# Threshold search of a router: the missed bit kept in PSUM and folded into the next candidate by one operation

## The reference

```python
probs = softmax(einsum('bsd,ed->bse', x, choice_w), axis=-1)
G, I = jax.lax.top_k(jnp.swapaxes(probs, -1, -2), k)
x_in = take_along_axis(x[:, None, :, :], I[..., None], axis=2)
h = silu(einsum('bekd,edf->bekf', x_in, w1))
x_mlp = einsum('bekf,efd->bekd', h, w2)
out = zeros_like(x).at[b_idx, I].add(G[..., None] * x_mlp)
```

## Time and profile before

| what | value |
|---|---|
| median of 3 runs | 2411.73 us (2411.46 to 2414.36) |
| profiled execution | 2411.47 us, of which the span from first to last instruction is 2409.6 us |
| PE (TensorE) busy | 2364.5 us, 98% of the span |
| DVE (VectorE) busy | 1401.0 us, 58% |
| ACT (ScalarE) busy | 839.1 us, 35% |
| POOL (GpSimd) busy | 1106.8 us, 46% |
| mean granted clock of TensorE | 0.996 |

### The profile page before, as it was taken

How to read it: one execution, slowest core, us unless ns; L and a number is a source line. 1 busy time by engine, 2 the same in 40 slices (tenths; PEclk the granted TensorE clock), 3 DMA queues, 4 the chain that set the end, 5 groups by cost and what they waited for, 6 DMA issues and landing times.

```text
span 2409.6 us, 34867 instructions
## 1 busy us (share of the span) xinstructions
PE 2364.5 (98%) x12586; PEld 2006.1 (83%) x12586; DVE 1401.0 (58%) x2730; ACT 839.1 (35%) x1470; POOL 1106.8 (46%) x980
## 2 busy tenths in 40 slices
PE   7999999999999999999999999999999999999997
PEld 6899978888999888888888888888888888888886
DVE  7777788967776888643543543543543544444433
ACT  4455444444454445322322322322223223223222
POOL 2000024400000246666566665665665665765765
PEclk9999999999999999999999999999999999999998
DMA  7555433445453434622522522522523423423322
GB/s 189 168 120 157 121 61 53 56 95 161 121 146 99 76 55 70 152 51 45 121 48 46 119 47 45 120 45 48 120 44 53 116 44 64 104 46 72 94 44 44
DMA packets 128139, 209.66 MB, mean 87 GB/s; under 512 B 28728, under 2 KB 53944, under 8 KB 127808
## 3 DMA queue, kind: packets, MB, share of 16 engines
q0 software_dynamic: 57728, 119.09, 27.6%
q1 hardware_dynamic: 70336, 89.68, 12.9%
HBM read 124.54 MB, written 100.93 MB: 94 GB/s over the span
## 4 chain that ended last, share of the span: by engine, by line
PE 93%; DVE 5%; ACT 1%; issue 1%; DMA 1%; POOL 0%; SPq 0%; DVEq 0%; ACTq 0%; POOLq 0%
PE ps L1291 30%; PE ps L1292 29%; PE ps L1293 29%; PE ps L1387 2%; PE ps L1519 1%; PE ps L1318 1%; DVE work L1229 0%; DVE thr L1141 0%; DVE stats L785 0%; DVE work L1212 0%; DMA xo<-in_L_attn_x_dram 0%; DMA normed_rows<-xo 0%; DVE qT L1004 0%; PE ps L1505 0%; DVE xT_lo L846 0%
## 5 line engine op out<-in xcount | busy, mean ns | idle before, releaser
L449 POOL DMA_INDIRECT rows<-normed_rows,idx_row x528 | 563.7, 1068 | 209.0 <-issue 209.0
L1291 PE MATMUL ps<-xi_hi,w_hi 128*128 128x512 f32 x1024 | 404.3, 395 | 0.0
L1291 PE MATMUL ps<-w_hi,h_hi 128*128 128x512 f32 x1024 | 402.3, 393 | 0.0
L1292 PE MATMUL ps<-xi_lo,w_hi 128*128 128x512 f32 x1024 | 400.4, 391 | 0.0
L1292 PE MATMUL ps<-w_lo,h_hi 128*128 128x512 f32 x1024 | 399.4, 390 | 0.0
L1293 PE MATMUL ps<-w_hi,h_lo 128*128 128x512 f32 x1024 | 399.1, 390 | 0.0
L1293 PE MATMUL ps<-xi_hi,w_lo 128*128 128x512 f32 x1024 | 398.7, 389 | 0.0
L1259 DVE CAST h_hi<-hf 128x512 fp32r<-128x512 f32 x256 | 111.5, 436 | 411.2 <-ACT hf L748 410.9
L546 POOL DMA_INDIRECT out_dram<-y,idx x128 | 221.4, 1730 | 273.1 <-ACT y L767 260.3
L748 ACT ACTIVATE hf<-ps 128x512 f32<-128x512 f32 x256 | 153.1, 598 | 519.4 <-PE ps L1293 519.4
L1293 PE MATMUL ps<-wq_hi,xT_lo 128*128 128x256 f32 (+2 forms) x768 | 246.4, 321 | 0.0
(11 more groups left out here) (174 smaller groups left out, 4217.4 us busy)
## 6 DMA issues: line engine op xcount, KB each, us to landing
w_raw<-in_L_ffn_w_dram SPq DMA_DIRECT2D x36, 512.0 KB, 8.1
w_raw<-in_L_ffn_w_dram SPq DMA_DIRECT2D x9, 2048.0 KB, 9.1
xo<-in_L_attn_x_dram SPq DMA_DIRECT2D x32, 512.0 KB, 4.5
normed_rows<-xo SPq DMA_DIRECT2D x32, 512.0 KB, 4.7
out_dram<-bo POOLq DMA_DIRECT2D x16, 1024.0 KB, 9.2
out_dram<-xo POOLq DMA_DIRECT2D x64, 256.0 KB, 3.9
xn<-normed_rows SPq DMA_DIRECT2D x96, 128.0 KB, 2.4
rows<-normed_rows,idx_row POOLq DMA_INDIRECT x528, 2.6
```

What stands on the lines that cost most here:

```text
L449: nc.gpsimd.indirect_dma_start(rows[:, tt, a, :], None, pieces[:, :], bass.IndirectOffsetOnAxis(ap=idx_row[:, b, tile, a:a + 1], axis=0)). ...
L1291: nc.tensor.matmul(dst, a_hi, b_hi, start=start, stop=False, skip_group_check=True)
L1292: nc.tensor.matmul(dst, a_hi, b_lo, start=False, stop=False, skip_group_check=True)
```

## The change

`hit` is gone. Its place takes `miss`, the last column of PSUM bank 7, seen as int32: it holds the bit if the count fell short, and zero if it did not. The candidate is kept over the steps: it starts as the highest bit, and one operation makes the next one from it, `cand = (miss | bit[s+1]) ^ cand`, which takes the missed bit out and puts the next one in. Behind the last bit `thr = miss ^ cand`. Each step so has one VectorE instruction and one wait fewer (60 in the two batches), and of the operation that follows the test one tensor lies in PSUM.

```diff
             thr = sb("thr", [P, 1], I32)
             cand = sb("cand", [P, 1], I32)
-            hit = sb("hit", [P, 1], I32)
+        miss = ps[:, 7, 511:512].bitcast(I32)
...
                     me.did(nc.vector.tensor_copy(probT, ps[:, 7, 0:2 * P]))
-                    me.did(nc.vector.memset(thr[:, :], 0))
+                    me.did(nc.vector.tensor_copy(cand[:, :], bit[:, 0:1]))
                     me.wait()
...
                 def count(s):
-                    me.did(nc.vector.tensor_tensor(cand[:, :], thr[:, :], bit[:, s:s + 1], ALU.bitwise_or))
-                    me.wait()
                     nc.vector.tensor_scalar(mark, probT, cand[:, :].bitcast(F32), None, ALU.is_ge, ALU.add,
                                             accum_out=cnt[:, 0:1]).then_inc(route_dve, 1)
...
                 def settle(s):
                     dve.wait_ge(route_pe, b * ROUTE + s + 2)
-                    me.did(nc.vector.tensor_scalar(hit[:, :], ps[:, 7, 0:1], float(CAP) - 0.5,
-                                                   bit[:, NT + s:NT + s + 1].bitcast(F32), ALU.is_ge, ALU.mult))
+                    me.did(nc.vector.tensor_scalar(miss, ps[:, 7, 0:1], float(CAP) - 0.5,
+                                                   bit[:, NT + s:NT + s + 1].bitcast(F32), ALU.is_lt, ALU.mult))
                     me.wait()
-                    me.did(nc.vector.tensor_tensor(thr[:, :], thr[:, :], hit[:, :], ALU.bitwise_or))
+                    if s < BITS - 1:
+                        me.did(nc.vector.scalar_tensor_tensor(cand[:, :], miss, bit[:, s + 1:s + 2], cand[:, :],
+                                                              ALU.bitwise_or, ALU.bitwise_xor))
+                    else:
+                        me.did(nc.vector.tensor_tensor(thr[:, :], miss, cand[:, :], ALU.bitwise_xor))
                     me.wait()
```

## The result

| | before | after |
|---|---|---|
| median of 6 runs | 2412.1 us (2411.38 to 2414.36) | 2403.26 us (2401.38 to 2404.5) |
| ratio | | 0.9961, 95% interval 0.995 to 0.9972 |
| span of the profiled execution | 2409.6 us | 2401.7 us |
| both second stages | 318.18 us | 307.86 us |

What follows compares the result with a forecast made beforehand. TensorE, busy 98% of the span, bounds the kernel; only its second-stage waits for VectorE can give: 1.2 + 1.56 + 0.34 + 6.45 = 9.55 us, so 2402.0 us, range 2399.8 to 2404.5.

Steps and rivals of the forecast that it cites:

- the clock's term: First batch, step 2: with fewer TensorE waits before it, no fall of the clock to 0.50; 1.56 us.
- first batch to the end of step 1: VectorE's candidate operation no longer held by POOL's subtraction, so TensorE's transposes come earlier; 1.2 us.
- first batch, step 3: A held fold of the test's bit, which made the sums late, goes; 0.34 us.
- first batch, the rest: Late end of the last step and short waits of 0.2 us, left out though each may give something.
- second batch, steps 3 to 13: Of 7.70 us excess over 4.88 us steps, all but list work of 1.05 and 0.2 goes; 6.45 us.
- second batch, the rest: Steps 1 and 2 give nothing: the time saved is spent waiting for the same POOL subtraction.
- one story told four times: Second batch, steps 3 to 13: a held fold makes VectorE late, so later operations are held too; within 6.45 us.
- bound of 1.57: Upper bound in us for the test writing to PSUM, taken from the longest held single column.
- first rival: Pass over the values held instead, to POOL's subtraction's end; gain 1 us, 2410.7 us; 8 in 100.
- rule of the Trainium skill: VectorE and GpSimd share ports under an exclusive lock; tensor_scalar's accumulator form can't take the pair, so the sum stands.
- half-way case: Second batch, step 3: marks still held, half the gain; 2404.7 to 2406.3 us; 12 in 100.
- slower one: Each step: PSUM operand costs more than the port did; about 2421 us at the upper bound; 4 in 100.

Runs made afterwards that it cites:

- e1: Kernel before with only the test's result moved to PSUM, still three small operations a step; both second stages 314.70 us, ratio 0.9969.
- e2: Kernel before with the threshold in PSUM and the test's result in SBUF, three small operations a step; both second stages 307.87 us.
- e3: Changed kernel with miss in SBUF, so the operation behind the test reads two SBUF tensors; both second stages 312.73 us.
- e4: Kernel before with POOL's subtraction as two instructions of 256 elements in place of one of 512; both second stages 318.97 us.
- e8: Kernel before with POOL's subtraction in two instructions and a POOL wait between them; both second stages 310.95 us.
- e5: Changed kernel with VectorE made late once by about 1.5 us, in step 1 of the first batch; both second stages 310.23 us.
- e6: Changed kernel with VectorE made late once by about 1.6 us, in step 3 of the second batch; both second stages 310.51 us.
- e7: Changed kernel with the addition ahead of the division in the form that also writes an accumulator; both second stages 306.52 us.

## Why the prediction was right, and where it was off

The mechanism was right, and shown: the hold follows the pair of SBUF tensors (e1, e2, e3), not the number of operations (e2), and it ends with POOL's instruction, or with the second of two that overlap (e4, with one exception; e8). One premise of the clock's term was wrong (below). By the terms of the sum, all from the two profiles of the first comparison:

| term | forecast | measured |
|---|---|---|
| first batch to the end of step 1 | 1.2 | 9.28 - 8.11 = 1.17 |
| first batch, step 2, clock | 1.56 | 6.44 - 4.90 = 1.54 |
| first batch, step 3 | 0.34 | 5.22 - 4.86 = 0.36 |
| first batch, the rest | left out | 135.73 - 135.08 = 0.65 |
| second batch, steps 3 to 13 | 6.45 | 61.38 - 54.82 = 6.56 |
| second batch, the rest | 0 | 0.04 |
| sum | 9.55 | 10.32 |

The least certain term, the clock's, came as forecast, and e5 shows that it hangs on the idle time in step 1. But the reason I gave for it was off, and some luck is in it. I had expected two of TensorE's three waits to go, and less idle time than the second batch has. The last wait stayed at 1.27 us (1.31 before), because TensorE came to it earlier too; the other two shrank, from 1.40 to 1.07 and from 0.33 to nothing listed. That makes 2.34 us, more than the 2.08 us (1.02 and 1.06) of the second batch before, which I had measured it by. It was still 0.7 us less than the first batch had before, and the clock didn't fall. The 1.2 us too lie elsewhere in part: 0.24 of the 1.17 came ahead of the first transposes (3.55 to 3.31 us from the turning of the probabilities) and 0.93 in step 1. In the second batch the same 0.24 was gained and 0.25 lost again in step 1 to the hold of L1224, as forecast.

The one story told four times is shown for its first and largest part by e6. Step 11, 2.01 us of the 6.56, has e1 beside it, where an earlier VectorE alone brought 1.96. The other holds of the second batch were not taken one by one.

Small things were off. The new operation takes 0.22 us, not 0.20, the upper of the two rows; the test is at 0.23 with a write to PSUM, 0.01 over before, so the bound of 1.57 was far too wide. The copy that fills the first candidate wasn't held, though it ran at 335.17 inside L486 (334.71 to 336.00). In step 1 of the first batch VectorE came to L1224 earlier than I had worked out and was held for some 0.57 of its 0.73 us, not 0.2; the time came out right because the hold's end and not its start sets it. What I left out, 0.65 us, is the last step (5.50 to 5.09 us) and a pitch of 4.873 in place of 4.883 us over 26 steps: a step in which TensorE shows no wait was not quite free of VectorE.

The first rival, the hold moving on to the pass over the values, falls: 60 executions at 0.466 to 0.483 us, 39 of them begun inside L486. The rule of the Trainium skill that I had weighed ("SBUF — State Buffer", "Who interferes with whom") holds in this case, and e7 shows it for a second operation (64 executions, none over 0.166 us). The half-way case and the slower one didn't come; the first would have needed the marks 1.5 us later, and e6 shows what it would have cost, 2.68 us. In pricing the slower one I said that nothing is held in the steps 14 to 30 of the second batch, and that VectorE waits up to 0.89 us there. But L1223 stands in every step from 887 us on (0.32 to 1.00 us), and about half of the waits are 0.3 us, so the 1.1 us at which I let the loss begin had no good ground; no run tests it. The whole time is 0.7 us short of the forecast gain while the second stages give 0.8 more than it; both medians have scatter of 3 us, and the ratio's interval, 6.8 to 12.1 us, holds either.

## What to carry to other kernels

An operation on one column that takes a microsecond is not slow, it stands: look which POOL instruction ends when it ends, and give it one tensor in PSUM or the accumulator form. What such a hold costs isn't its length. Where the engine that sets the pace shows no wait, 1.2 us a step were worth 0.01; at one place a delay of 1.2 us cost nothing and one of 1.6 us, which brought VectorE's work in behind POOL's, cost 2.7. Read the price from the steps' pitch between two rows of the engine that sets it, rather than from its listed waits, and take a program's own undisturbed stage as the ruler when the whole scatters.

## What the runs showed that I had not expected

- A hold was mostly not released between two POOL instructions that follow each other without a wait: 1.25 us over both halves, and 35 of 36 held folds ended with a second half. The one release came where their recorded times overlap by 0.03 us and not by 0.3; why it came there was not tested. With a wait of POOL between them it was 0.69 us.
- A plain copy of one column from SBUF to SBUF ran unheld inside POOL's subtraction (0.144 us, both executions), where a plain `tensor_scalar` of 16 columns stood for up to 0.995 us.
- The lock works in the other direction too: POOL's subtraction took 2.07 us in place of 1.59 when VectorE's marks had started 0.30 us ahead of it.
- 0.7 us of TensorE's waits more or less in one step decided over 1.54 us of clock in the next: before, e1 and e5 have waits of 3.0 us and then a step of 6.44 to 6.45 us, changed, e3 and e7 waits of 2.1 to 2.3 us and then 4.88 to 4.90.
